# Perceiver layer with a routed feed-forward: ten early one-hot columns, four bias products behind slot 0's transposes, three tile sums added while the expert rows load

## The reference

```python
x = x + xattn(layernorm(x), ctx)      # cross attention, 16 heads, 257 context rows for each batch
x = x + attn(layernorm(x))            # causal self attention, 16 heads
x = x + ffn(layernorm(x))

def ffn(x):                           # 8 experts, the best 2 for each token
    logits = x @ gate_w.T + gate_b
    gate = softmax(where(in top 2, logits, -inf))
    return sum_e gate[e] * (x @ expert_w[e] + expert_b[e])
```

## Time and profile before

| | |
|---|---|
| median of 3 runs | 793.52 us (792.46 to 793.53) |
| the profiled execution | 790.52 us, of which span 788.7 us |
| PE busy | 767.9 us (97%) |
| DVE busy | 489.8 us (62%) |
| ACT busy | 340.4 us (43%) |
| POOL busy | 216.2 us (27%) |
| mean clock granted to PE | 0.985 of full speed |

### The profile page before, as it was taken

One profiled execution on the slowest core, in us unless ns is written; L12 is line 12 of the kernel. 1 busy time (PEld: TensorE's weight loads), 2 busy tenths in 40 slices (PEclk: granted clock), 3 DMA queues, 4 the chain that ended last, 5 costly groups with the idle time before them and its releaser, 6 DMA issues. The chain is left out here.

```text
span 788.7 us, 21576 instructions
## 1 busy us (share of the span) xinstructions
PE 767.9 (97%) x9062; PEld 647.7 (82%) x9063; DVE 489.8 (62%) x1130; ACT 340.4 (43%) x816; POOL 216.2 (27%) x192
## 2 busy tenths in 40 slices
PE   8999999999999999999999999999899999699997
PEld 7888888888888888888889888898677777578884
DVE  6656565565656556656465655857789998822236
ACT  5533544334453344533445334544556674123330
POOL 0222223222233222332222322222123321146640
PEclk9999999999999999999999999999999999889999
DMA  8722001100011000110000101111753227645548
GB/s 298 271 80 89 28 29 50 34 28 30 28 39 44 29 29 29 36 48 28 29 28 28 55 28 30 41 69 55 295 228 140 115 95 276 263 136 171 182 130 315
DMA packets 22445, 78.11 MB, mean 99 GB/s; under 512 B 3248, under 2 KB 3760, under 8 KB 19408
## 3 DMA queue, kind: packets, MB, share of 16 engines
q1 hardware_dynamic: 18528, 64.45, 22.4%
q0 software_dynamic: 3680, 12.06, 4.7%
q10 hardware_dynamic: 144, 0.26, 0.1%
HBM read 58.15 MB, written 18.61 MB: 97 GB/s over the span
## 5 line engine op out<-in xcount | busy, mean ns | idle before, releaser
L161 PE MATMUL bank<-chi,wparts 128*128 128x258 f32 x496 | 143.7, 290 | 0.0
L163 PE MATMUL bank<-chi,wparts 128*128 128x258 f32 x496 | 140.1, 282 | 0.0
L162 PE MATMUL bank<-clo,wparts 128*128 128x258 f32 x496 | 140.0, 282 | 0.0
L334 POOL TENSOR_TENSOR pdiag_hi<-p_last_and_rinv_hi,const 128x256 fp32r<-128x256 f32 x32 | 19.7, 617 | 328.4 <-DVE p_last_and_rinv_hi L581 328.4
L328 POOL TENSOR_TENSOR ksin<-kb,const 128x1032 f32<-128x1032 f32 x32 | 95.0, 2969 | 41.7 <-ACT kb L381 41.7
L786 PE MATMUL bank<-wparts,chi 128*128 128x512 f32 x256 | 105.7, 413 | 0.0
L161 PEld LDWEIGHTS bank<-chi,wparts 128*128 128x128 f32 x496 | 93.5, 189 | 12.8 <-issue 12.8
L787 PE MATMUL bank<-wparts,chi 128*128 128x512 f32 x256 | 101.5, 397 | 0.0
L788 PE MATMUL bank<-wparts,clo 128*128 128x512 f32 x256 | 101.1, 395 | 0.0
L373 ACT ACTIVATE chi<-craw 128x1032 fp32r<-128x1032 f32 x32 | 34.2, 1069 | 146.3 <-PE bank L788 144.2
L557 DVE TENSOR_TENSOR v<-bank,bias_cross 128x512 f32<-128x512 f32 x64 | 43.9, 688 | 83.9 <-PE bank L788 83.9
(11 more groups left out here) (335 smaller groups left out, 1684.5 us busy)
## 6 DMA issues: line engine op xcount, KB each, us to landing
craw<-ctx_t_dram SPq DMA_DIRECT2D x32, 516.0 KB, 3.4
expert_lo<-weights_dram SPq DMA_DIRECT2D x8, 1024.0 KB, 13.2
expert_hi_scratch<-wraw SPq DMA_DIRECT2D x16, 512.0 KB, 2.9
wparts<-expert_hi_scratch SPq DMA_DIRECT2D x8, 1024.0 KB, 9.5
wraw<-weights_dram SPq DMA_DIRECT2D x7, 1024.0 KB, 5.6
expert_lo<-ffn_out_scratch SPq DMA_DIRECT2D x16, 256.0 KB, 5.4
x<-x_dram SPq DMA_DIRECT2D x8, 256.0 KB, 7.7
out_dram<-x SPq DMA_DIRECT2D x8, 256.0 KB, 2.2
```

The costliest lines, as they stand in the source:

```text
L161: pe.matmul(psum, ahi(c), bhi(c), start=(c == 0), stop=False)
L162: pe.matmul(psum, ahi(c), blo(c), start=False, stop=False)
L163: last = pe.matmul(psum, alo(c), bhi(c), start=False, stop=(c == chunks - 1))
```

## The change

- `ON_R` goes from 8 to 10. The groups of place one-hots are (0,5), (5,10), (10,13), (13,16) instead of (0,4), (4,8), (8,10), (10,13), (13,16). All of them go to `kbd`; the tokens go to one tile. Both early groups are built one behind the other ahead of DVE's additions to the last tile. `max` of tile 6 moves behind the last tile's statistics (`bn_stats`), and its `max_index` behind the variance (in place of the second group).
- `gather_row` is computed before `spare`, and POOL waits for `s_rows` 1 last instead of first.
- PE transposes the gates before slot 0. Behind slot 0's transposes come the bias products of tiles 0 to 3 (`first_bias_products`), which wait for the transposed gates and for `s_rows` 3. ACT copies the gates before `slot_hi(0)`. The wait for the biases' own loads (`s_eb`) moves ahead of all this.
- At the end PE adds both late slots to the banks of tiles 0, 1 and 2 first, without bias products in between, and then goes tile by tile. DVE adds these three banks to `x` before the loaded choices.

```diff
-ON_R = 8
+ON_R = 10
...
-            tokens_late = carve(K2 - ON_R, PAIRS)
+            tokens = carve(K2, PAIRS)
...
+            at_place = kbd
+            place_groups = ((0, 5), (5, 10), (10, 13), (13, 16))
...
-            TAIL_ADDS = ([(t, k) for k in range(2) for t in (0, 1)] + [(0, 3), (1, 3)]
-                         + [(t, k) for k in range(2) for t in (2, 3)] + [(t, k) for k in range(2) for t in (4, 5)]
-                         + [(2, 3), (3, 3), (WITH_X, 2), (4, 3), (5, 3), (WITH_X, 3)])
+            EARLY_SUMS = 3
+            TAIL_ADDS = ([(t, 3) for t in range(EARLY_SUMS)] + [(t, k) for k in range(2) for t in (0, 1)]
+                         + [(t, k) for k in range(2) for t in (2, 3)] + [(3, 3)]
+                         + [(t, k) for k in range(2) for t in (4, 5)]
+                         + [(4, 3), (WITH_X, 2), (5, 3), (WITH_X, 3)])
...
+                pool.wait_ge(s_x3pad, 16)
+                pool.wait_ge(s_x3d, 16 * TILES)
                 pool.wait_ge(s_rows, 1)
-                pool.wait_ge(s_x3d, 16 * TILES)
-                pool.wait_ge(s_x3pad, 16)
...
-                slot_hi(0, 0)
                 for i in range(2):
                     act.wait_ge(s_gtp, i + 1)
                     act.activation(gates_t[i], gates_bank[i][:, 0:P], ACT.Copy).then_inc(s_gt, 1)
+                slot_hi(0, 0)
...
-                place_onehots(*place_groups[0])
-                top(T - 2)
+                for group in place_groups[:2]:
+                    place_onehots(*group)
...
+                dve.wait_ge(s_lg, T - 1)
+                dve.max(top8[:, T - 2, :], logits[:, T - 2, :]).then_inc(s_top, 1)
                 dve.wait_ge(s_stats3, T + 2)
...
-                place_onehots(*place_groups[1])
+                dve.wait_ge(s_top, T - 1)
+                dve.max_index(idx8[:, T - 2, :], top8[:, T - 2, :], logits[:, T - 2, :]).then_inc(s_idx, 1)
                 logits_evac(T - 1)
...
                 dve.tensor_scalar(second, number, B * S + 0.5, -float(B * S), ALU.is_ge, ALU.mult).then_inc(s_rt, 1)
+                dve.wait_ge(s_rt, 27)
+                dve.scalar_tensor_tensor(gather_row[:], number, 1.0, second, ALU.max, ALU.add).then_inc(s_rows, 1)
                 dve.scalar_tensor_tensor(spare, number, 0.0, rc(R_SPARE, SLOTS), ALU.is_equal, ALU.mult).then_inc(s_rt, 1)
                 dve.wait_ge(s_rt, 28)
-                dve.scalar_tensor_tensor(gather_row[:], number, 1.0, second, ALU.max, ALU.add).then_inc(s_rows, 1)
...
-                def tile_sums():
+                def first_bias_products():
 
                     pe.wait_ge(s_gt, 2)
-                    pe.wait_ge(s_eb, 64)
+                    pe.wait_ge(s_rows, 3)
                     for t in range(4):
                         bias_product(t)
-                    pe.wait_ge(s_exlo, SLOTS)
-                    bias_product(4)
-                    bias_product(5)
+
+                def tile_sums():
+
                     pe.wait_ge(s_late_lo, 1)
                     pe.wait_ge(s_yev, SLOTS - 1)
-                    bias_product(6)
                     pe.wait_ge(s_late_onehot, LATE)
-                    for t in range(4):
+                    for t in range(EARLY_SUMS):
                         add_late(0, t)
                     pe.wait_ge(s_late_lo, LATE)
                     pe.wait_ge(s_yev, SLOTS)
+                    for t in range(EARLY_SUMS):
+                        add_late(1, t).then_inc(s_sums, 1)
+                    for t in range(EARLY_SUMS, ON_PE):
+                        if t >= 4:
+                            bias_product(t)
+                        add_late(0, t)
+                        last = add_late(1, t)
+                        if t == WITH_X:
+                            last = add_rows(t, x[:, t, :], True)
+                        last.then_inc(s_sums, 1)
                     bias_product(ON_PE)
...
+                pe.wait_ge(s_eb, 64)
+                gates_transposed()
                 slot_transposed(0, 0, 0)
-                gates_transposed()
+                first_bias_products()
```

More of the change, by code:

```diff
@@ L1088, in perceiver @@
             WITH_X = ON_PE - 1
-            TAIL_ADDS = ([(t, k) for k in range(2) for t in (0, 1)] + [(0, 3), (1, 3)]
-                         + [(t, k) for k in range(2) for t in (2, 3)] + [(t, k) for k in range(2) for t in (4, 5)]
-                         + [(2, 3), (3, 3), (WITH_X, 2), (4, 3), (5, 3), (WITH_X, 3)])
-            FIRST_ADD, SECOND_ADD, FINAL_ADD = ({t: n + 1 for n, (t, k) in enumerate(TAIL_ADDS) if k in which}
-                                                for which in ((0,), (1, 2), (3,)))
+            EARLY_SUMS = 3
[3 more added lines that the diff above has]
+                         + [(4, 3), (WITH_X, 2), (5, 3), (WITH_X, 3)])
+            ADDED = {t: [n + 1 for n, (u, _) in enumerate(TAIL_ADDS) if u == t] for t in range(ON_PE)}
             gates_bank = (b_av, b_xt)
@@ L1159, in _ @@
                     else:
-                        sp.wait_ge(s_choices, FINAL_ADD[t])
+                        sp.wait_ge(s_choices, ADDED[t][-1])
                     sp.dma_start(out[t * P:(t + 1) * P, :], x[:, t, :]).then_inc(s_stored, 16)
@@ L1527, in place_in_tile, with place_onehots @@
                                              ALU.add).then_inc(s_rt, 1)
-                def place_onehots(k0, k1, into):
-                    dve.tensor_tensor(into, place[:, k0:k1].unsqueeze(2).to_broadcast([P, k1 - k0, P]),
+                def place_onehots(k0, k1):
+                    dve.tensor_tensor(at_place[:, k0:k1, :], place[:, k0:k1].unsqueeze(2).to_broadcast([P, k1 - k0, P]),
                                       rc(R_IOTA, P).unsqueeze(1).to_broadcast([P, k1 - k0, P]),
@@ L1727, in _ @@
                 token = rc(R_TOKEN, K2).unsqueeze(2).to_broadcast([P, K2, PAIRS])
-                for n, (k0, k1, into) in enumerate(((0, ON_R, tokens), (ON_R, K2, tokens_late))):
+                for n, (k0, k1, into) in enumerate(((0, ON_R, tokens[:, 0:ON_R, :]), (ON_R, K2, tokens[:, ON_R:K2, :]))):
                     dve.tensor_tensor(in_tile[:, k0:k1, :], rc(R_IOTA, PAIRS).unsqueeze(1).to_broadcast([P, k1 - k0, PAIRS]),
@@ L1790, in late_output_lo, with after_the_last_add_to, add_choice @@
                                              late_hi[j].bitcast(F32), ALU.mult, ALU.subtract).then_inc(s_late_lo, 1)
-                def add_first(t):
+                def after_the_last_add_to(t, n):
+                    if n > ADDED[t][0]:
+                        dve.wait_ge(s_choices, max(m for m in ADDED[t] if m < n))
+                def add_choice(t, k):
                     dve.wait_ge(s_half[t // 2], 64)
-                    dve.tensor_tensor(x[:, t, :], halves[:, 2 * t, :], x[:, t, :], ALU.add).then_inc(s_choices, 1)
-                def add_second(t):
-                    dve.wait_ge(s_choices, FIRST_ADD[t])
-                    dve.tensor_tensor(x[:, t, :], halves[:, 2 * t + 1, :], x[:, t, :], ALU.add).then_inc(s_choices, 1)
+                    dve.tensor_tensor(x[:, t, :], halves[:, 2 * t + k, :], x[:, t, :], ALU.add).then_inc(s_choices, 1)
                 def add_both(t):
@@ L1827, in _ @@
                     late_output_lo(j)
-                for t, add in TAIL_ADDS:
-                    (add_first, add_second, add_both, add_sum)[add](t)
+                for n, (t, add) in enumerate(TAIL_ADDS):
+                    after_the_last_add_to(t, n + 1)
+                    if add < 2:
+                        add_choice(t, add)
+                    elif add == 2:
+                        add_both(t)
+                    else:
+                        add_sum(t)
             @block.tensor
@@ L2024, in _ @@
                 pe.wait_ge(s_xo, TILES + 1)
-                for n, (k0, k1, onehots) in enumerate(place_groups):
+                for n, (k0, k1) in enumerate(place_groups):
                     pe.wait_ge(s_at_place, n + 1)
@@ L2029, in _ @@
                     for j in range(k0, k1):
-                        columns = tokens[:, j, :].bitcast(F32) if j < ON_R else tokens_late[:, j - ON_R, :]
-                        last = narrow(b_cp[:, 0:PAIRS], at_place(j), columns, j == 0, j == K2 - 1)
+                        last = narrow(b_cp[:, 0:PAIRS], at_place[:, j, :], tokens[:, j, :], j == 0, j == K2 - 1)
                 last.then_inc(s_table, 1)
@@ L2034, in _ @@
                 for j in range(K2):
-                    last = narrow(b_v[:, 0:SLOTS], at_place(j), slot_gates[:, j, :], j == 0, j == K2 - 1)
+                    last = narrow(b_v[:, 0:SLOTS], at_place[:, j, :], slot_gates[:, j, :], j == 0, j == K2 - 1)
                 last.then_inc(s_table, 1)
```

8 lines of the change are left out of this document (removed).

## The result

The changed kernel takes 798.27 us (median, 797.01 to 798.85), the kernel before 792.97 (791.73 to 793.53): ratio 1.0066, 95% interval 1.0053 to 1.0079. It is 5.3 us slower, where 1.4 faster than that median, 791.6, was forecast. The profiled execution took 798.41 (span 796.6).

The account below looks back on a forecast made before the run. It took PE's routing before slot 0, at 1.2 GHz, and DVE's additions at the end as bounds. Gains of 0.9 and 1.05 from 790.52 gave 788.57, plus 3.00 carried over 791.57 us; range 790.0 to 793.5.

Parts of the forecast that it names:

- Part 1: Logits of the last tile on DVE: could start earlier, limited by POOL's power; gain 0.30 us, bounds 0.15 and 0.45.
- Part 2: Table product on PE: with ten early columns PE ends 0.33 us earlier, DVE's compares 0.34; taken as 0.30.
- Part 3: POOL's first gather: rows ready 0.69 us earlier, but ACT's store lands last at 687.8; lead 0.50.
- Part 4: PE before product 0: gates hidden, bias group 1.9 us, clock back at 694.9 saves 1.03; parts 1 to 4 together +0.9.
- Rival 3: Between slots 0 and 1: bias matmuls run one behind the other, 4.5 to 6.8 us; 794.4 or 796.7; chance 0.06.
- Rival 1: First slots: clock returns when it did, at 697.4 or later; front -0.3, time 792.8 us; chance 0.20.
- The rule on switching the tiling mode: Ahead of product 0: two added switches drain the engine, 0.2 to 0.6 us at low clock; front +0.3 to +0.7.
- Part 5: The end: three early sums, DVE done at 784.0 instead of 785.4, last store at 784.85; gain 1.05 us.
- The sum: Whole kernel: 790.52 - 0.9 - 1.05 = 788.57 us, plus 3.00 from profiled execution to median: 791.57; chance 0.47.

Follow-up runs that it names:

- e6: The kernel before, unchanged, run and profiled once more: 793.17 us, ratio 0.9998.
- e5: The changed kernel without the early bias group; bias products 0 to 3 side by side behind the last slot, 4 to 7 behind the early sums: 792.82 us, ratio 0.9992.
- e7: The kernel before with POOL's first row gathers held until VectorE has copied the third row of slots: 795.19 us, ratio 1.0020.
- e12: The same kernel as e7, run once more for its profile: 794.66 us, ratio 1.0024.
- e4: The changed kernel with the bias products of tiles 4 to 7 side by side behind the sums of tiles 0 to 2: 796.62 us, ratio 1.0057.
- e9: e5's kernel with 6 and 7 extra matmuls of 128 rows in PE's two idle stretches ahead of the first table product: 793.49 us, ratio 1.0009.
- e10: e9's kernel with 5 more extra matmuls between the two table products: 794.08 us, ratio 1.0007.
- e14: The kernel before with the new order of sums and bias products 4 to 7 side by side behind the sums of tiles 0 to 2: 788.69 us, ratio 1.0005.

## Why the prediction was wrong, step by step

**Part 1, logits +0.30: right in direction, a little small.** From the last gate product (678.63 before, 678.38 after) to the last logits it is 1.78 before and 1.32 after: 0.46. The power on POOL took 0.55 and not 0.93, the exception that the step had named.

**Part 2, the table +0.30: right.** From the logits to DVE's first reading of the table 7.29 before, 6.95 after: 0.34. The first product runs through its 128 instructions without a stop.

**Part 3, POOL's first gather, lead 0.50, store as the new wait: too large and for the wrong reason.** From the gate product 10.02 before, 9.86 in e6, 9.59 after: a lead of 0.3 to 0.4, although `gather_row` is 0.9 earlier. The store was issued at 681.56 and landed 5.2 later, at 686.8, 1.2 ahead of POOL's start. What the profiles show instead is a longer step: six have the new order of waits. In five of them POOL begins 1.09 to 1.10 us behind `gather_row`'s start, with the store landed 1.1 to 1.9 us ahead of POOL. Only in e5 does the store land last, as forecast, at 687.3, 0.5 behind that start, and the step is 1.34. The nine with the old order, e7 and e12 aside, have 0.48 to 0.80. The new order seems to cost some 0.5; it was not tried alone.

**Part 4, the bias group: the step that failed first.** Its length was right (1.9 forecast, 2.02 measured). Two things were not. First the cover: the gates were to hide in the wait for gather 0, with table 2 ended at 691.27. In 11 of the 17 profiles the stops make PE late there and not the gather; after, the table ends at 694.55, PE waits for no rows behind it, and gates and group lie on the path in full. Second the clock: "if it comes back as long after as before, that is 694.9". PE had no gap from 693.69 on, and the clock came back at 703.6, 9.9 us later. That absence of gaps brings the clock back 3.0 us later was drawn from one execution's two events and does not hold. From the gate product to slot 2's transposes the change lost 0.03 + 3.35 against e6 where the forecast for all four parts gained 0.9. Part 4 itself had put the group at a loss of 0.3 without an earlier return of the clock, because slot 1's rows were to come late anyway; with the stops they were there, and the loss is the whole group. Rival 3 had named the place and the sign, but its mechanism (matmuls one behind the other) did not happen: they ran four abreast. Rival 1, no earlier return, allowed for a return at 697.4 or later, but priced only 697.4.

The rule on switching the tiling mode weighed little: from 695.95 to 697.97 there is no gap at either border, and the first wave takes 0.16 more than the second (1.22, 1.06). The drain that the Trainium skill (TensorEngine Tiling (Array Packing), section Tiling Modes) speaks of is at most that here.

**Part 5, the end, +1.05: the second failed step.** "The late link is now load, PE, ACT, store" took PE to be idle at 782.1. The part takes off the seven bias products ahead of 771.40 and counts the early additions and DVE's 17, but never puts products 4 to 6 back, which now stand alone behind the sums, like product 7. Before, products 0 to 6 took 1.92 (769.48 to 771.40), and product 7, which stood alone before too, 1.05:

```profile
773.47 1.12 PE L2048 MATMUL quad<-sm,craw 8*128 8x512 f32 x2
774.52 1.19 PE L2052 MATMUL quad<-wparts 128*128 128x512 f32 x4
```

That is 2.97 in all. After, four single products take 4.2 and more, so PE has more to do here and not less; side by side the four are 1.07. Its last product of loaded rows starts 18.16 behind the load's issue (773.49 to 791.65), before 14.75. Of the 3.4 us between, some 1.3 are this work and some 1.7 the clock's fall (0.83 over 10 us is 3.4 us at half speed), which the forecast did not have. What the part said of DVE did hold: three sums at 777.97 to 779.8, nearly all in its idle time. With the products in waves (e4, e5, e9, e10, e14) the end is 20.4 to 20.9 and once 21.6 (e9), against 21.0 to 22.2 in the nine profiles with the old one: 0.6 less in the middle of each, about half of the forecast 1.05. The median of e14 shows none of it; its interval allows up to 0.9.

**The sum.** The profile shown was an execution without stops, 3.00 below the median, and the difference was "carried over" as if the change could not touch it. It was no constant: e6 has 1.5 us more from the gate product to slot 2's transposes and 1.6 more from there to the load. The stops in the table product decide whether there is a wait to hide work in. What the changed kernel does in executions without stops was not tried.

## What to carry to other kernels

Work moved "behind" a wait is free only if the wait is there in most executions: profile the kernel again when its profiled time lies below its own median, and look at whether the same engine is still late. Before narrow matmuls are moved, price them as they will stand: here four side by side cost 1.07 us and one alone 1.05, and at the low clock double. Don't count on the clock coming back sooner because an idle gap is closed.

## What the runs showed of the hardware that was not expected

A run of small matmuls (128x32 by 23 columns) stops for about 0.41 us after every 3 to 6 instructions, for some 4 us, on two chips while row gathers are in flight (ten profiles; the changed kernel's has them too), and not with the gathers held back (two profiles) or on the third chip (three). Keeping TensorE busy ahead of the table (e9) moved the fall of the clock by some 7 us and halved the low stretch, without gain. The clock stays low, or falls, while PE is busy all the time: it is at 1.2 GHz for 9.9 us behind 693.69 in the changed kernel, and it falls in the ten full us from 780 (granted clock 0.83). The fall at the end stands in all three profiles with single products on 8 rows among wide additions and in none of the others; that the narrow products cause it is likely and not shown.
